# Second attention: the second projected head of each pair scaled by ScalarE and added by GpSimd

## The reference

```
x = x + tanh(g_xattn[0]) * attention_0(layernorm(x), ctx, ...)   # 16 heads of 16
x = x + tanh(g_ffn[0])   * moe_0(layernorm(x), ...)              # 16 experts, 8 chosen
x = x + tanh(g_xattn[1]) * attention_1(layernorm(x), ctx, mask, ...)
x = x + tanh(g_ffn[1])   * ternary_ffn_1(layernorm(x), ...)

attention_1: q = (t @ Wq) in 16 heads of 128; k, v = ctx @ Wk, ctx @ Wv in 8 heads, each for two q heads
             out = softmax(mask(q @ k.T / sqrt(128))) @ v;  return concat(out) @ Wo
```

## Time and profile before

| | us |
|---|---|
| median of three runs | 1571.52 (1571.43 to 1574.1) |
| profiled execution | 1572.19 |
| its span in the profile | 1570.9 |
| TensorE busy | 1378.6 (88%) |
| VectorE busy | 1248.3 (79%) |
| ScalarE busy | 1106.1 (70%) |
| GpSimd busy | 780.8 (50%) |

### The profile page before, as it was taken

How to read it: one execution, slowest core, us unless ns; L and a number is a source line. 1 busy time by engine, 2 the same in 40 slices (tenths; PEclk the granted TensorE clock), 3 DMA queues, 4 the chain that set the end, 5 groups by cost and what they waited for, 6 DMA issues and landing times.

```text
span 1570.9 us, 25673 instructions
## 1 busy us (share of the span) xinstructions
PE 1378.6 (88%) x8430; PEld 682.5 (43%) x8524; DVE 1248.3 (79%) x2335; ACT 1106.1 (70%) x2028; POOL 780.8 (50%) x664
## 2 busy tenths in 40 slices
PE   5688798887887888789889989899998999999989
PEld 4243243343333234234445544455454545454545
DVE  5666667677677445769998888989899899999887
ACT  4656665864864665568778878778877787887764
POOL 4014013213213013238777658887697776676763
PEclk9798898999998999999999999999999999999999
DMA  4001300200242010010000000000010000000000
GB/s 165 1 1 29 58 1 1 50 15 1 43 129 83 2 54 1 6 43 22 6 1 1 1 22 22 7 1 22 1 27 1 28 3 26 10 19 1 1 1 28
DMA packets 20491, 36.71 MB, mean 23 GB/s; under 512 B 4898, under 2 KB 15238, under 8 KB 19334
## 3 DMA queue, kind: packets, MB, share of 16 engines
q1 hardware_dynamic: 20358, 35.07, 7.7%
HBM read 26.53 MB, written 1.15 MB: 18 GB/s over the span
## 4 chain that ended last, share of the span: by engine, by line
PE 33%; DVE 9%; issue 8%; POOL 4%; ACT 3%; DMA 0%; DVEq 0%; ACTq 0%; POOLq 0%
PE BK L713 32%; DVE arena L1696 4%; POOL arena L2092 3%; DVE arena L1677 2%; ACT arena L1954 1%; DVE arena L1710 1%; ACT arena L1947 1%; ACT arena L1965 0%; DVE arena L2280 0%; ACT L1947 0%; POOL arena L2089 0%; DMA arena<-in_wup 0%; POOL arena L1087 0%; DVE arena L998 0%; DVE arena L2286 0%
## 5 line engine op out<-in xcount | busy, mean ns | idle before, releaser
L713 PE MATMUL BK<-arena 128*128 128x512 bf16 (+12 forms) x8100 | 1332.5, 366 | 156.2 <-DVE arena L1514 40.9
L713 PEld LDWEIGHTS BK<-arena 128*128 128x128 bf16 (+6 forms) x8194 | 645.7, 110 | 812.5 <-issue 167.9
L2092 POOL TENSOR_TENSOR arena<-arena 128x512 f32<-128x512 f32 (+1 forms) x352 | 509.7, 1448 | 133.8 <-ACT arena L1947 108.9
L1696 DVE TENSOR_TENSOR arena<-arena 128x512 bf16<-128x512 f32 (+1 forms) x416 | 485.7, 1171 | 29.3 <-ACT arena L1954 28.2
L1947 ACT ACTIVATE arena<-BK,arena 128x512 f32<-128x512 f32 (+1 forms) x416 | 286.2, 688 | 125.2 <-PE BK L713 105.3
L1845 ACT ACTIVATE arena<-BK 128x512 f32<-128x512 f32 (+1 forms) x416 | 227.1, 603 | 97.2 <-PE BK L713 91.8
L1514 DVE TENSOR_REDUCE arena<-BK 128x1 f32<-128x512 f32 x384 | 244.5, 684 | 60.9 <-PE BK L713 59.9
L1954 ACT CAST arena<-arena 128x512 bf16<-128x512 f32 (+1 forms) x416 | 253.6, 610 | 0.0
L1677 DVE CUSTOM_DVE_ANT_0 arena<-BK,arena 128x512 bf16<-128x512 f32 (+1 forms) x256 | 145.3, 568 | 23.7 <-PE BK L713 21.1
L1965 ACT ACTIVATE arena<-BK 128x512 bf16<-128x512 f32 (+1 forms) x256 | 129.5, 508 | 45.5 <-PE BK L713 44.3
L2003 POOL TENSOR_TENSOR arena<-arena 128x256 f32<-128x256 f32 (+6 forms) x45 | 30.2, 670 | 188.1 <-ACT arena L1782 185.8
(11 more groups left out here) (178 smaller groups left out, 857.8 us busy)
## 6 DMA issues: line engine op xcount, KB each, us to landing
arena<-arena SPq DMA_DIRECT2D x144, 50.0 KB, 2.2
arena<-in_ctxT SPq DMA_DIRECT2D x8, 800.5 KB, 4.3
arena<-in_ctxk SPq DMA_DIRECT2D x4, 768.0 KB
arena<-in_wo SPq DMA_DIRECT2D x1, 2048.0 KB, 7.6
arena<-in_wqT SPq DMA_DIRECT2D x1, 2048.0 KB, 8.9
arena<-in_x SPq DMA_DIRECT2D x4, 256.0 KB, 9.9
arena<-in_rsel SPq DMA_DIRECT2D x1, 1024.0 KB, 9.6
arena<-in_rw1T SPq DMA_DIRECT2D x1, 1024.0 KB, 5.2
```

The source lines that it names most:

```text
L713: return T.matmul(out_, lhsT, rhs, start=start, stop=stop, skip_group_check=True)
L1696: V.tensor_tensor(Pl[k][0:m, :], P1[k][0:m, :], Ph[k][0:m, :], ALU.subtract).then_inc(p_low, 1)
L2092: G.tensor_tensor(acc[0:m, g % 2, :], acc[0:m, g % 2, :], P1[k][0:m, :], ALU.add).then_inc(summed1, 1)
```

## The change

Head j = 0 stays as it was. For head j = 1 VectorE does nothing; ScalarE scales both token tiles from PSUM into a new tile `ys` (128x512, float32) and frees the bank, and GpSimd adds `ys` to both token tiles at once and counts `added`. ScalarE's next use of `ys`, VectorE's addition of the next group's head 0 and the norm statistics of a batch wait for `added`; VectorE's old waits for the other head's bank go.

```
+        ys = sb("ys", [128, 512], F32, SM)
...
 dve_norm_stats, turn 3:
-                    dve.wait_ge(*emptied("o1p", 8 * b + 7, 1))
+                    dve.wait_ge(added, 8 * b + 8)
...
+        added = sem("added")
...
 vector_main:
-                elif kind == "o1p":
+                elif kind == "o1p" and arg[1] == 0:
                     g, j = arg
                     dve.wait_ge(full[i], n + 1)
                     dve.wait_ge(gated, g + 1)
                     if g:
-                        dve.wait_ge(*emptied("o1p", g - (j == 0), 1 - j))
+                        dve.wait_ge(added, g)
...
 scalar_main:
+                elif kind == "o1p" and arg[1]:
+                    g, j = arg
+                    act.wait_ge(full[i], n + 1)
+                    act.wait_ge(gated, g + 1)
+                    if g:
+                        act.wait_ge(added, g)
+                    for t2 in range(2):
+                        t = A.activation(ys[:, 256 * t2:256 * t2 + 256], BK[i][:, 256 * t2:256 * t2 + 256], ACT.Identity,
+                                         scale=dn[:, 10 + t2:11 + t2])
+                    t.then_inc(free[i], 1)
...
 gpsimd_main:
+                elif kind == "o1p" and arg[1]:
+                    g, j = arg
+                    pool.wait_ge(*emptied("o1p", g, 1))
+                    pool.wait_ge(*emptied("o1p", g, 0))
+                    k = 2 * (g // 8)
+                    G.tensor_tensor(x_sb[:, k:k + 2, :].rearrange("p t d -> p (t d)"), x_sb[:, k:k + 2, :].rearrange("p t d -> p (t d)"),
+                                    ys[:, :], ALU.add).then_inc(added, 1)
```

## The result

The changed kernel takes 1583.69 us, median of five runs (1580.07 to 1585.84), against 1571.52 (1570.22 to 1574.1) in five of the kernel before: ratio 1.0066, 95% interval 1.0036 to 1.0097, slower. The forecast was 1577 in 1563 to 1592, slower as the likeliest sign. The profiled execution took 1585.68 us (span 1584.4), 13.5 more than the one before. Lines have moved: L1696 is now L1698, L1710 L1712, L1947 L1949, L2089 L2101, L2092 L2104, L2098 L2110, L983 L984; the scaling is L1975, the addition L2116.

What follows compares the result with a forecast made beforehand. The prediction took TensorE to bound the second attention, with only 55.7 us of excess where VectorE's relief could pay. Terms -3.7 + 1.6 + 4.3 + 1.9 + 1.2 + 1.3 = +6.6 us on 1571.5 gave 1577, 8 in 10 within 1563 to 1592.

Steps and rivals of the forecast that it cites:

- (a): Second attention: VectorE loses two of four additions per group, priced by halved chain share at -3.7 us (0 to -24).
- (b): Second attention: ScalarE gains two 128x256 scalings per group, 0.5 us each, no table load; +1.6 us (0 to +15).
- (c): Second attention: GpSimd gains one 128x512 addition per group, priced by the sums' chain share; +4.3 us (0 to +39).
- (d): Second attention: VectorE's subtractions wait longer for the added GpSimd instructions, 14 us, of which +1.9 reaches the time.
- (e): New waits: each batch's norm statistics, three times in the stage, wait for the addition; +1.2 us.
- (f): End of the second attention, where nothing covers it: last scaling and addition delay the statistics; +1.3 us (+0.5 to +2.5).
- VectorE's time comes back: Rival: some 12 of 27 slow groups give back 0.88 us each; -8 us, 1563; chance 0.27.
- 0.45 us of VectorE's time per GpSimd instruction: Second attention: waiting that each GpSimd instruction gives VectorE's subtractions; 31 added ones make 14 us.
- first rival: The rival that VectorE's time comes back in slow groups: -8 us, 1563; chance 0.27.
- the shared access is full: Rival: VectorE and GpSimd fill their shared SBUF access, so additions lengthen groups; +20 to +39 us, 1590 to 1611; chance 0.15.
- Hidden on both sides: Rival: TensorE covers clean groups, gain and loss cancel in the others; 1571.5 within 3 us; chance 0.21.

Runs made afterwards that it cites:

- e3: Kernel before with VectorE's two second-head additions cut to one of 128x4, nothing put in their place: 0.9967, 1566.9 us.
- e11: Kernel before plus ScalarE's two scalings alone, from an SBUF tile into scratch that nobody reads: 0.9981, 1572.04 us.
- e1: Kernel before plus one GpSimd 128x512 scratch addition per group, on which nothing waits: 1.0068, 1583.84 us.
- e2: Changed kernel with GpSimd's addition cut to 2 of 256 columns of each token tile: 0.9965, 1567.62 us.
- e5: Null: kernel before with only the new tile, the semaphore and one memset at the stage's start: 1.0008, 1577.0 us.
- e12: Changed kernel with GpSimd's addition over the first token tile only, 128x256 in place of 128x512: 0.9986, 1571.98 us.
- e8: Changed kernel timed once more, unaltered, beside experiments on another chip: 1.0039, 1578.3 us.
- e6: Kernel before plus two GpSimd memsets of the 128x512 scratch per group, in place of e1's addition: 0.9998, 1575.83 us.
- e7: Changed kernel with the new scheme in 23 groups; VectorE keeps the second head in those beside splits and masks and the last: 1.0035, 1580.03 us.
- e9: Changed kernel with the new scheme only in groups 4, 5, 6, 13, 14, finished beside clean groups: 0.9973, 1568.45 us.
- e10: Changed kernel with the new scheme only in groups 20 to 27, finished beside ternary weights: 0.9986, 1574.44 us.
- e4: Changed kernel with most groups' GpSimd addition put off to just before the next group's first sum: 1.0037, 1579.04 us.

## Why the prediction was right

The sum of +6.6 (which makes 1578; the forecast rounded it down to 1577) was met by +6.6 outside the groups whose clock dips, and by +8.0 with them. Whole runs say 0.66% and 0.39%, 10.4 and 6.1 us, and both intervals hold 6.6 and 8.0. The terms:

| term | predicted | measured | by |
|---|---|---|---|
| (a) VectorE relieved, in the stage | -3.7 | -3.0 (and -0.7 at the end), for 21 of the 28 us | e3 |
| (b) scalings | +1.6 | -0.2 | e11 |
| (c), (d) addition, in the stage | +6.2 | +6.9 (e1); 7.9 (change less e2) | e1, e2 |
| (e) norm waits | +1.2 | 0.0 | groups 8, 16, 24 |
| (f) end | +1.3 | +1.5 (0.4 of it as worked out) | timeline of after |

That the sum is met so closely is luck: (b) and (e) were put 3 us too high together, and the addition 0.7 to 1.7 us too low. What held is the sign, from the two large terms: a relief worth little, an addition worth more.

(a) The share of the chain held by an instruction was a good price for taking it away, in this one case. The room for it was put too high: 55.7 us of the stage beyond TensorE's own work rest on a trace that lacks matmuls, and e5 has 825.0 - 775.6 = 49.4. "VectorE's time comes back" (-8) is refuted: even with nothing added only 3.7 come back.

(b) Missed by size. I priced 0.05 us per us of ScalarE, but the scalings stand where ScalarE idles (e11), and the instructions whose shares I used for the price stand elsewhere. The duration was right: 0.5 forecast, 473 ns. No table load came.

(c) and (d) Right together, wrong apart. The step "0.45 us of VectorE's time per GpSimd instruction" failed: e1 adds 32 of them and L1698 gains 0.9 us in all, 0.03 each; changed kernel less e2 is 6.6 us, 0.21 each. The 15.2 us by which L1698 did get slower, near my 14, are to 8.6 there without any addition (e2), since VectorE, relieved, arrives earlier at a subtraction that still waits for GpSimd. The prediction says this against its first rival, but (d) put all of the growth down to the addition. The agreement was luck. In its place the runs show the sums and the gate late on GpSimd (the waits under e1), and in the ternary groups VectorE's L1737 and L1742 held up by the addition, which I had not looked at. So (d) should have been near nothing and (c) about 7 to 8; that size is read off e1 and e2 afterwards, and nothing in the trace of before gives it. The chain's share doesn't: the sums hold 4.3 to 4.7 points more of it in e1 and in the changed kernel and nothing more in e2, but in e12, which is 6 us cheaper than the changed kernel by the estimate above, they hold 10.5% (690 to 1535 us) where the changed kernel has 9.9. Nor do single waits add up to it: those shown under e1 are 21.1, 8.5 and 4.2 us in e12.

(e) L984 waited 3.1 us for the addition in 4 places, 1.38 of them at the end of the stage; but groups 8, 16 and 24, which hold the other norms, kept their 33.9, 27.5 and 26.9 us.

(f) Right in size, half by luck. The statistics start only 0.4 us later, since the scaling doesn't follow head 0 but runs beside it (1536.26 and 1536.24). The other 1.0 comes from the sums and subtractions that wait for each other in turn at the stage's end, with the addition of group 30 ahead of them. The last group loses 0.9 more, which no term held; how is not shown (e1, with an addition there too, has -0.2).

Clean groups stayed at 24.0, which refutes "the shared access is full" there: that rival asked for 1.27 us in half of the groups or more, and only five come near it: 3, 11, 19 and 31 with +0.9 or +1.0, and 12 with its dip. "Hidden on both sides" holds in the clean groups alone. The forecast of 1577 was 6.7 us below the median; by e8's median of 1578.3 it was 1.3 below. The intervals of 1.0066 and 1.0039 overlap, and I have no cause for the difference but the scatter ahead of the stage.

Open: why the clock falls after the same waits in one execution and not in another, and whether the change makes it likelier in group 12. It fell there in both profiles of the changed kernel and in those of e1, e2, e3, e6, e7 and e12, and, of the profiles with VectorE and GpSimd as before in groups 9 to 12, in two of five (e9 and e10, not before, e5 and e11); in e4 it didn't, and the group lost 0.9 us at 1.00. So all of the 1.6 may be the change's, and the change would then cost 8.0. Open too is how much of the addition's price in the stage is that it reads and how much that it takes GpSimd's time. No version here with the whole computation beats the kernel before.

## What to carry to other kernels

Count what an engine's relief is worth and what the new work costs apart, each by a kernel of its own: here -3.7 against +10, though only 28 us of busy time left the busier engine (21 in the run that gave -3.7) and 52 came to the idler one, which had half of the span free. An engine at 50% busy is no free place where there are stretches in which it is nearly full (24.6 of 27.6 us in a group with splits), and where others wait for what it does next. What is dropped from a comparison for its disturbance can hold the cost itself, as group 11 did. A busy time that grows in an engine need not be a cost, and one that matches the forecast need not have the forecast's cause.

## What the runs showed of the hardware

- A GpSimd addition of 128x512 float32 takes 1262 ns alone and 1638 in the mean beside VectorE's subtractions. One that begins under a subtraction ends 1.13 us after it; a subtraction that begins under a GpSimd sum ends 0.55 us after that.
- VectorE's tensor_scalar L1737 has one SBUF tensor as input (128x512, float32 to bf16), yet it lasts from 471 to 1501 ns, and where it meets the addition 895 to 915 for 481. The same section of the Trainium skill's "SBUF — State Buffer" names tensor_scalar among the operations that can take the pair shared with GpSimd; this row agrees. The prediction's sentence that VectorE instructions with one SBUF input don't contend leaves this exception out.
- A GpSimd memset of 128x512 float32 takes 525 ns and does not slow VectorE's two-input subtraction beside it (672 to 679 ns, with 670 the shortest of all).
- ScalarE's scaling with a per-partition factor, 128x256: 473 ns from PSUM, 504 from SBUF.
